# A fused attention and feed-forward block: another order of the work, the first quarter split in its bank, and the last two masks added by VectorE

## The chip, the cores and the metric
One core of a Trainium2 chip. The metric is the device time of one execution in microseconds (us). TensorE multiplies, VectorE, ScalarE and GpSimd work on elements, and SyncE's queue issues the DMAs. PSUM is the memory that TensorE writes, in banks of 128 x 512 f32; SBUF is the memory for the rest.

## The reference
With x of 2 x 1024 tokens and C = 128, all in f32:
```
xn  = layernorm(x)
q3, k3 = xn @ Wq.T, xn @ Wk.T              # 8 heads of 3 dimensions
v   = xn @ Wv.T                            # 8 heads of 16
scores = (q3 . k3) * scale + (q3 . dir_h) * (k3 . dir_h)
attn = softmax(where(causal, scores, -inf));  A = (attn @ v) @ Wo.T
h   = bitlinear(xn, w_fc) + gate * (xn @ v'.T @ fast_b.T @ u.T)
F   = bitlinear(relu(h)**2, w_proj)        # ternary weights times a scale, hidden size 512
out = x + A + F
```

## The kernel before
**Tiling.** The 2048 tokens are four quarters of 512. Attention is made in eight chunks: batch, group of four heads, and which half of the batch's tokens the queries are (`CHUNKS`). Chunks 0, 1, 6 and 7 have queries in a first half (four steps of 128 keys, all crossing the diagonal, of 512, 384, 256 and 128 queries), chunks 2 to 5 in a second half (four full steps of 512, then four such).

**A chunk.** Its `max` units make scores on TensorE (queries on the partitions, K=32 rows of bf16, line 875), and VectorE takes their least values: a plain reduce where no mask is needed (line 576), and an addition of `mask_row` with a reduce (line 579) on the diagonal. (The scores are negated, so that a minimum stands for the softmax's maximum.) Chunks 0, 1, 6, 7 have 12 units, the others 28, of which 16 are plain ones. `top` and `prep` write the minima as three bf16 parts beside the queries, and a transpose (`maxT`) puts them on the other axis. Then for each step and pair of heads `st` (line 903) makes the scores with the keys on the partitions and the maximum subtracted, ScalarE takes the exponential (line 729), and `pv` (line 927, 8 matmuls in f32) adds to `obank`. `oT`, `oB` and `y` turn, divide and project.

**The diagonal, in chunks of `BOUNDED`** (all eight before): scores over the diagonal could overflow, so ScalarE first applies a Relu to the first 128 columns of both heads of the pair (`late`, line 715), and after the exponential GpSimd sets what lies over the diagonal to zero (`causal`, line 446); `pv` waits for GpSimd. In a chunk outside `BOUNDED`, VectorE adds the tile `late` (a large number over the diagonal) to the scores in their bank, and `pv` waits for the exponential alone.

**q and k** are split in three bf16 parts each (`qkv`, `split`, `spread`), and laid in the tile X with repeats. For quarters 1 to 3 GpSimd does it and a DMA transposes X. For quarter 0 the path is: ScalarE casts the first part (line 675), VectorE subtracts it from the bank into the SBUF tile `rest` (line 528), casts that (532), subtracts again (534), and ScalarE and VectorE copy the parts to X (691, 539); TensorE transposes X (`rows`, line 842), and ScalarE copies the result to QK (695).

**The feed-forward part**: `ffn`, `ffn2` (lines 850, 855; 2 matmuls of 128x512 in f32 each), Relu, square on GpSimd, and `hid` (763), which shares its bank with `y`.

**The order.** Each engine runs its items in the order of one list, `ORDER`. `WEAVE` is that list with a letter for each stream (M maxima, A `st`, O `late` of bounded chunks, K `late` of the others, G exponentials, D `causal`, P `pv`, H `ffn`, B `hid`, Y `oB` and `y`, and so on); each letter takes the next item of its stream. Engines wait for each other by semaphores only. The `max` units have three banks (`VB`), `st`, `ffn` and `qkv` two double banks (`AB`). `IDLE` puts matmuls on zeros ahead of four items of TensorE's (12 before `weights wqk`, 7 before `xT 0`, 2 before `qkv 0`, 6 before `rows 0 0`); they don't wait for the item's own operands.

Of the kernel before, what the change touches and what calls it, by code (L numbers as in the profile page):

```python
# [21 lines left out]
G = H // HG  # L22
# [83 lines left out]
BOUNDED = (0, 1, 2, 3, 4, 5, 6, 7)  # L106
# [65 lines left out]
NNWNNWCXFNUNWQCFIULNENVUNNMMEMHMMMNHSMMXMJMXQIVMMQNLHMMEVMMHRMMHMMHMMTXMJMMAOMHMGMHMMSMMRAAMOMMGOHGMAIMMOHMGMM  # L172
AMOAMGMMMAOOTMGMGDAAODMOGMMGAOMAMMPMDDMGMOAPMGSAOSGPOLRMGMAMADOTGOPADGOMMPDGHMMHMQVMMADMAPEIMAMPMAMMAMPAMPPJLM
AAMPAOMGMAOMEMAMMPMGMADORGPMOGAOMMMADPGMOMAGMAPOOGMMGTADMADMAMMAMAMSMAMAMMAMMAMMAOMOPGGMAMMOGMAPDPOAPMGMMROAGO
PDTAGPAMMOGODGMAPMMAAMPADMMMAPMAMAMPAMMPPMAMPHOMGHHMMHMAMMOPMMAMGOPRMMAPMGMOAPMMGOADPGOGAMTMOADOGBSGAAYMBAYMAD
PAMDMMPPAMPBAAMBAMYOAPGOGMAPOSGRMAOMPDMMGAPAOTDMGMOMGAOPAGPOGMAMADOBODPPGARGBDYABOSGYOAGOAPOGBBATGDAOYOGBAGAOP
ODDGBAGDOPABGPYOPGPAOAOGGYBAOYGDAPPDPOGDPBPBBYYY
# [23 lines left out]
def build(nc, x, Wq, Wk, Wv, Wo, scale, fast_b, w_fc, w_proj, u, v, gate, consts, out):  # L201
# [3 lines left out]
    with ctx:  # L205
# [258 lines left out]
        def _(dve):  # L464
# [12 lines left out]
            for item in ORDER:  # L477
# [36 lines left out]
                elif item == ("xn", 0):  # L514

                    dve.wait_ge(rstd_ready, 1)
                    for n in range(TPC):
                        last = nc.vector.tensor_scalar(xn[:, n, :], x_sb[:, n, :], mv[:, n, 0:1], rstd[:, n:n + 1],
                                                       ALU.subtract, ALU.mult)
                    last.then_inc(xn_ready, 1)  # L520
                elif item == ("weights", "wqk"):
                    nc.vector.tensor_copy(wall[:, C:VQK], filled(item)[:, 0:2 * NQ]).then_inc(free(item), 1)
                elif kind == "qkv":
# [111 lines left out]
        def _(act):  # L635
# [9 lines left out]
            for item in ORDER:  # L645
# [31 lines left out]
                elif kind == "v":  # L677
# [4 lines left out]
                    act.wait_ge(res_ready, q + 1)  # L682
                    if q == 0:
                        act.wait_ge(ones_ready, 1)
                    nc.scalar.copy(V[:, q * TPC:(q + 1) * TPC, :, 0:HD],  # L685
                                   qkv_view(unit)[:, :, 0:C].rearrange("p n (h d) -> p n h d", d=HD)).then_inc(free(unit), 1)
                elif item == ("spread", 0):
                    for k, ready in ((0, hi_ready), (1, mid_ready)):
                        act.wait_ge(ready, 1)
                        for side in range(2):  # L690
                            last = nc.scalar.copy(*part_rows(0, side, k))
# [285 lines left out]
```

## Time and profile before
| | |
|---|---|
| runs | 171.37 us (median of 170.3, 171.37, 173.21) |
| the profiled execution | 172.44 us, its span 169.8 us |
| TensorE busy | 155.9 us |
| VectorE busy | 133.6 us |
| ScalarE busy | 123.0 us |
| GpSimd busy | 67.5 us |
| mean granted clock of TensorE | 0.91 |

The span goes from the first to the last instruction of the profiled execution. The granted clock is 1.00 at 2.4 GHz and 0.50 at 1.2 GHz. "Busy" for TensorE includes matmuls that overlap in the pipeline.

### The profile page before, as it was taken

Reading aid. Unit: us, or ns where it says so; the run is one execution under the profiler, and the core shown is the slowest. Engines: PE = TensorE matmul, PEld = TensorE weight load, DVE = VectorE, ACT = ScalarE, POOL = GpSimd, SP = SyncE. Lnnn points to the kernel's source line nnn. Section 1 sums busy time; section 2 is a strip of 40 time slices with the busy share of each in tenths; the row PEclk is TensorE's granted clock in tenths of the full one; section 3 lists DMA queues with packets and bytes.
Section 4 is the critical chain, followed back from the end, with each engine's and each line's share of the span. In section 5 each row is a group of like instructions: output and inputs, shape, how many; then the busy total and the mean of one; then the engine's idle time right before and its main releaser. Section 6 shows DMA issues by size and latency. Waiting matters only on the chain.

```text
span 169.8 us, 3241 instructions
## 1 busy us (share of the span) xinstructions
PE 155.9 (92%) x1080; PEld 63.1 (37%) x1081; DVE 133.6 (79%) x435; ACT 123.0 (72%) x218; POOL 67.5 (40%) x119
## 2 busy tenths in 40 slices
PE   6995999898879988898889999999999999999993
PEld 2452627232212124232122221242255523785772
DVE  0899659899999899899999796899995867150541
ACT  1556764858578674999889776986879898969810
POOL 8064004999415992702450151000492223832310
PEclk9999559999975599999995558999999999999999
DMA  3850000060100016090100010000011020021012
GB/s 96 201 180 2 0 0 4 0 124 2 31 0 8 0 31 124 0 127 0 31 0 4 0 33 2 0 4 0 0 35 31 0 66 0 0 62 37 11 52 62
DMA packets 16764, 5.76 MB, mean 34 GB/s; under 512 B 11308, under 2 KB 16620, under 8 KB 16748
## 3 DMA queue, kind: packets, MB, share of 16 engines
q1 hardware_dynamic: 16352, 5.41, 14.8%
q10 hardware_dynamic: 396, 0.16, 0.3%
q8 instruction: 8, 0.13, 0.3%
q14 instruction: 8, 0.07, 0.1%
HBM read 2.02 MB, written 1.05 MB: 18 GB/s over the span
## 4 chain that ended last, share of the span: by engine, by line
PE 54%; DVE 31%; ACT 8%; issue 3%; DMA 2%; SPq 1%; ACTq 0%; DVEq 0%
PE obank L927 16%; DVE pm L576 11%; DVE vbank L579 10%; PE vbank L875 9%; PE vbank L763 9%; PE abank L903 6%; ACT Pr L729 6%; PE abank L850 5%; PE abank L855 4%; DMA k_sb<-in_consts 2%; PE vbank L947 2%; ACT abank L715 2%; DVE pm L579 2%; DVE stats L484 1%; PE abank L842 1%
## 5 line engine op out<-in xcount | busy, mean ns | idle before, releaser
L729 ACT ACTIVATE Pr<-abank 128x1024 f32<-128x1024 f32 (+3 forms) x96 | 74.5, 814 | 6.9 <-PE abank L903 1.9
L579 DVE CUSTOM_DVE_ANT_0 vbank<-vbank,mask_row 128x128 f32<-128x128 f32 (+3 forms) x128 | 58.8, 523 | 7.9 <-PE vbank L875 7.6
L875 PE MATMUL vbank<-QK 32*128 32x512 bf16 (+3 forms) x192 | 47.5, 364 | 3.4 <-DVE pm L576 1.7
L927 PE MATMUL obank<-Pr,V 128*32 128x512 f32 (+3 forms) x384 | 43.5, 544 | 0.2 <-issue 0.2
L576 DVE TENSOR_REDUCE pm<-vbank 128x1 f32<-128x512 f32 x64 | 39.5, 681 | 3.2 <-PE vbank L875 3.0
L446 POOL TENSOR_SCALAR_AFFINE_SELECT Pr<-Pr 128x512 f32<-128x512 f32 x32 | 20.1, 637 | 49.9 <-ACT Pr L729 49.6
L903 PE MATMUL abank<-QK 32*128 32x512 bf16 (+3 forms) x192 | 33.9, 358 | 3.2 <-ACT Pr L729 1.9
L875 PEld LDWEIGHTS vbank<-QK 32*128 32x128 bf16 x192 | 12.5, 94 | 49.7 <-issue 20.1
L715 ACT ACTIVATE abank<-abank 128x256 f32<-128x256 f32 x64 | 23.6, 375 | 9.8 <-PE abank L903 9.0
L437 POOL TENSOR_TENSOR r<-r 128x1024 f32<-128x1024 f32 x8 | 15.1, 1895 | 11.4 <-ACT r L709 11.4
L579 DVE DVE_READ_ACCUMULATOR2_ANT pm<- 128x1 f32 x128 | 18.0, 141 | 0.0
L763 PE MATMUL vbank<-w2T,r 128*128 128x128 f32 x128 | 17.5, 284 | 0.0
L903 PEld LDWEIGHTS abank<-QK 32*128 32x128 bf16 x192 | 8.7, 92 | 22.0 <-ACT Pr L729 13.4
L763 PEld LDWEIGHTS vbank<-w2T,r 128*128 128x128 f32 x128 | 15.3, 191 | 2.8 <-issue 2.4
L709 ACT ACTIVATE r<-abank 128x1024 f32<-128x1024 f32 x8 | 8.2, 1024 | 9.0 <-PE abank L855 9.0
L927 PEld LDWEIGHTS obank<-Pr,V 128*32 128x32 f32 x384 | 8.8, 113 | 11.6 <-issue 9.9
L611 DVE STREAM_TRANSPOSE oT<-obank 128x512 f32<-128x512 f32 x8 | 5.7, 710 | 7.1 <-PE obank L927 7.1
L850 PE MATMUL abank<-xnT,w1T 128*128 128x512 f32 x16 | 9.8, 700 | 0.6 <-ACT V L685 0.4
L456 POOL CAST X<-nmax 128x16 bf16<-128x16 f32 x8 | 2.1, 257 | 20.6 <-DVE nmax L595 16.8
L631 DVE TENSOR_TENSOR xn<-vbank,x_sb 128x256 f32<-128x256 f32 x8 | 3.4, 424 | 8.5 <-PE vbank L947 8.4
L855 PE MATMUL abank<-xnT,w1T 128*128 128x512 f32 x16 | 9.8, 698 | 0.0
L769 PE MATMUL obank<-mask_row 128*128 128x512 bf16 x26 | 7.9, 445 | 1.3 <-POOL mask_row L388 1.3
(101 smaller groups left out, 127.8 us busy)
## 6 DMA issues: line engine op xcount, KB each, us to landing
x_sb<-in_L_attn_x SPq DMA_DIRECT2D x4, 256.0 KB, 3.6
out_y<-xn SPq DMA_DIRECT2D x8, 128.0 KB, 1.8
wfc_sb<-in_L_ffn_w_fc SPq DMA_DIRECT2D x1, 256.0 KB, 4.1
wpj_sb<-in_L_ffn_w_proj SPq DMA_DIRECT2D x1, 256.0 KB, 3.0
QK<-X SPq DMA_TRANSPOSE x10, 2.5
k_sb<-in_consts SPq DMA_DIRECT2D x2, 64.0 KB, 3.2
Wv_sb<-in_L_attn_Wv ACTq DMA_DIRECT2D x1, 64.0 KB, 3.5
Wo_sb<-in_L_attn_Wo ACTq DMA_DIRECT2D x1, 64.0 KB, 4.0
```

Source lines behind the costliest of these rows:

```text
L437: nc.gpsimd.tensor_tensor(r, r, r, ALU.mult).then_inc(r2_ready, 1)
L446: nc.gpsimd.affine_select(diagonal, diagonal, [[0, HG], [1, P]], ALU.is_ge, 0.0, base=0, channel_multiplier=-1).then_inc(causal_done, 1)
L576: last = nc.vector.tensor_reduce(out=least, in_=s_n, op=ALU.min, axis=AX.X)
L579: last = nc.vector.tensor_tensor_reduce(out=s_n, in0=s_n, in1=mask_row[:, CH - keys:CH], scale=1.0, scalar=3.0e38, op0=ALU.add, op1=ALU.mi ...
L715: nc.scalar.activation(scores, scores, ACT.Relu).then_inc(bounded, 1)
L729: nc.scalar.activation(Pr[:, n % PSLOTS, 2 * pair:2 * pair + 2, 0:cols], src[:, :, 0:cols], ACT.Exp, scale=-1.0).then_inc(free(unit), 1)
L763: nc.tensor.matmul(o[:, at:at + P], r2[:, j, t:t + P], w2T[:, j, :], start=j == 0 and at == 0, stop=False)
L850: nc.tensor.matmul(o[:, 0, :], w1T[:, j * P:(j + 1) * P], xnT[:, q * CH:(q + 1) * CH], start=True, stop=True)
L855: nc.tensor.matmul(bank(unit)[:, 1, :], w1T[:, j * P:(j + 1) * P], xnT[:, q * CH:(q + 1) * CH], start=True, stop=True).then_inc(full(unit), 1)
L875: last = nc.tensor.matmul(o[:, at:at + keys], QK[r, quarter(b, chunk), 0, g, q0:q0 + P], QK[r, quarter(b, half), 1, g, 0:keys], start=True ...
L903: last = nc.tensor.matmul(o[:, n, 0:cols], QK[r, quarter(b, j // TPC), 1, g, k0:k0 + P], QK[r, quarter(b, chunk), 0, g, first:CH], start=T ...
L927: last = nc.tensor.matmul(obank[32 * h:32 * h + 32, first:CH], V[:, b * TPB + j, HG * g + h, :], Pr[:, n % PSLOTS, h, 0:cols], start=step ...
```

## The change
Four edits.

1. `BOUNDED` loses chunks 6 and 7. Their 16 Relus of ScalarE (8 each) become 16 additions of VectorE in the banks, and their 8 `causal` items of GpSimd are gone.
2. The first quarter's split. VectorE's residual stays in the bank. ScalarE casts the middle part from there, with the copies of the first part to X before and behind it; VectorE subtracts the middle part from the bank. V's copy out of the bank waits for that.
3. `xn 0` releases its four tiles one by one, and the transposes of `xT 0` wait for each.
4. `WEAVE` is another list.

```diff
-BOUNDED = (0, 1, 2, 3, 4, 5, 6, 7)
+BOUNDED = (0, 1, 2, 3, 4, 5)
...
+        def qk_rest():
+
+            return qkv_view(("qkv", 0))[:, :, C:VQK].rearrange("p t (s c) -> p t s c", s=2 * G)
...
-                        last = nc.vector.tensor_scalar(xn[:, n, :], x_sb[:, n, :], mv[:, n, 0:1], rstd[:, n:n + 1],
-                                                       ALU.subtract, ALU.mult)
-                    last.then_inc(xn_ready, 1)
+                        nc.vector.tensor_scalar(xn[:, n, :], x_sb[:, n, :], mv[:, n, 0:1], rstd[:, n:n + 1],
+                                                ALU.subtract, ALU.mult).then_inc(xn_ready, 1)
...
-                    nc.vector.tensor_tensor(rest(q), src, bf16_part(q, 0),
+
+                    nc.vector.tensor_tensor(rest(q) if q else src, src, bf16_part(q, 0),
                                             ALU.subtract).then_inc(res_ready, 1)
                 elif item == ("split", 0):
-                    dve.wait_ge(res_ready, 1)
-                    nc.vector.tensor_copy(bf16_part(0, 1), rest(0)).then_inc(mid_ready, 1)
                     dve.wait_ge(mid_ready, 1)
-                    nc.vector.tensor_tensor(bf16_part(0, 2), rest(0), bf16_part(0, 1),
+                    nc.vector.tensor_tensor(bf16_part(0, 2), qk_rest(), bf16_part(0, 1),
                                             ALU.subtract).then_inc(lo_ready, 1)
...
-                    act.wait_ge(res_ready, q + 1)
                     if q == 0:
+                        act.wait_ge(lo_ready, 1)
                         act.wait_ge(ones_ready, 1)
+                    else:
+                        act.wait_ge(res_ready, q + 1)
...
+                elif item == ("split", 0):
+                    act.wait_ge(hi_ready, 1)
+                    nc.scalar.copy(*part_rows(0, 0, 0))
+                    act.wait_ge(res_ready, 1)
+                    nc.scalar.copy(bf16_part(0, 1), qk_rest()).then_inc(mid_ready, 1)
+                    nc.scalar.copy(*part_rows(0, 1, 0))
                 elif item == ("spread", 0):
-                    for k, ready in ((0, hi_ready), (1, mid_ready)):
-                        act.wait_ge(ready, 1)
-                        for side in range(2):
-                            last = nc.scalar.copy(*part_rows(0, side, k))
+                    act.wait_ge(mid_ready, 1)
+                    for side in range(2):
+                        last = nc.scalar.copy(*part_rows(0, side, 1))
                     last.then_inc(laid_act, 1)
```

What the new list does to TensorE's order at the places that matter (`max c u` is unit u of chunk c):
```
start, before: wqk | xT 0, lora_u, wvo, qkv 0, lora_b, rows 0 0, w1, max 0 0-1, rows 0 1, max 0 2, ffn 0, max 0 3-5, ffn2 0
start, after:  wqk | wvo, xT 0, lora_u, qkv 0, lora_b, rows 0 0, rows 0 1, max 0 0-1, w1, max 0 2-7, xT 1, max 0 8-9, xT 2,
               qkv 1, max 0 10-11, qkv 2, max 1 0-1, ffn 0, ...
chunk 2's maxima, before: ffn 4, ffn2 4 by unit 11, then units 12-27 with st of chunk 0 and 1, then pv 0 0
chunk 2's maxima, after:  ffn 3, 4 and their ffn2 by unit 14, pv 0 0 behind unit 19, pv 0 1 behind 22, pv 0 2 behind 26,
                          then max 3 0-9 with st of chunk 1, pv 0 3, st 2 0 0, max 3 10-11, qkv 3, max 3 12-13, st, pv 1 0
chunk 4's maxima, before: pv 2 1 to 2 4 by unit 8, then units 9-25 with st of chunk 3, pv 2 5, ..., pv 2 6, pv 2 7
chunk 4's maxima, after:  pv 2 1 to 2 5 by unit 14, then units 15-27 and max 5 0 with st of chunk 3, pv 2 6, pv 2 7
end, before: ... y 3 0, hid 2 0 0, st 7 3 0, y 3 1, st 7 3 1, pv 7 0-3, hid 2 0 1, hid 2 1 0, hid 2 1 1, y 2 0, y 2 1
end, after:  ... hid 2 0 0, st 7 2, pv 7 0-1, st 7 3, y 3 0, y 3 1, pv 7 2-3, hid 2 0 1, hid 2 1 0, hid 2 1 1, y 2 0, y 2 1
```
VectorE now has `rstd 1` behind `max 0 1` and not before `max 0 0`, and in chunks 6 and 7 the additions stand between `max 7 10`, `top 7`, `oT 5`, `y 1`, `oB 3` and `oT 6`, in the order of the scores. ScalarE has V's copy and `lora_b` ahead of the first `rows`.

## Rows read from the trace of the kernel before

**Rows 1.** Windows of the whole span: busy us (instructions) per engine, granted clock, DMA.
```profile
17.84:24.66 6.82, 6.82 (x27) 2.81 (x26) 4.29 (x24) 4.62 (x11) 0.00 (x0) 0.50 0.00 0
24.66:48.56 23.90, 21.53 (x101) 8.67 (x100) 22.64 (x70) 16.53 (x27) 15.63 (x26) 1.00 0.15 28
48.56:58.80 10.24, 9.67 (x48) 2.04 (x48) 9.98 (x37) 7.28 (x16) 6.65 (x8) 0.50 0.01 3
58.80:89.52 30.72, 27.05 (x210) 8.28 (x206) 29.12 (x71) 25.35 (x42) 14.09 (x29) 1.00 0.28 43
89.52:103.17 13.65, 13.49 (x76) 3.02 (x76) 11.70 (x41) 10.80 (x18) 2.91 (x7) 0.50 0.05 11
103.17:144.00 40.83, 40.25 (x345) 14.58 (x342) 34.44 (x119) 34.50 (x54) 11.29 (x19) 1.00 0.06 14
144.00:169.80 25.80, 23.03 (x228) 16.84 (x226) 8.83 (x21) 14.86 (x31) 8.01 (x14) 1.00 0.14 37
84.90:89.50 4.60, 4.09 (x27) 1.11 (x23) 4.60 (x8) 3.99 (x6) 2.50 (x2) 1.00 0.00 0
```

**Rows 2.** The chain that ended last, middle and end: start us, us, what.
```profile
79.90 9.74 DVE pm L576 x16
...
94.38 1.44 PE obank L927 x8
...
99.60 1.90 PE obank L927 x8
...
122.13 0.99 PE obank L927 x8
...
163.27 2.87 PE vbank L763 x24
```

**Rows 3.** Timeline of the start: start us, us, engine, line, operation.
```profile
6.37 1.69 PE L769 MATMUL obank<-mask_row 128*128 128x512 bf16 x7
...
7.36 0.29 POOL L398 COPY Wo_by_head<-Wo_sb 128x128 f32<-128x128 f32 x1 [3.03 <-DMA Wo_sb<-in_L_attn_Wo]
...
7.89 0.60 PE L821 MATMUL abank<-k_sb,xn 128*128 128x128 f32 x4
...
10.13 1.43 PE L831 MATMUL abank<-wall,xnT 128*128 128x176 f32 x8 [0.37 <-ACT wall L734]
...
11.60 0.32 ACT L675 CAST r<-abank 128x192 bf16<-128x192 f32 x1 [1.61 <-PE abank L831]
...
12.23 0.35 DVE L528 TENSOR_TENSOR r<-abank,r 128x192 f32<-128x192 f32 x1
...
12.62 1.08 DVE L532 CAST r<-r 128x192 bf16<-128x192 f32 x1
13.15 1.76 ACT L691 COPY X<-r 128x288 bf16<-128x288 bf16 x4
...
13.73 1.18 DVE L534 TENSOR_TENSOR r<-r 128x192 bf16<-128x192 f32 x1
...
16.29 1.01 ACT L695 CAST QK<-abank 128x1024 bf16<-128x1024 f32 x1 [1.38 <-PE abank L842]
...
17.23 1.56 PE L806 MATMUL vbank<-k_sb,wfc_sb 128*128 128x128 f32 x8
...
18.53 0.17 DVE L512 SCALAR_TENSOR_TENSOR shift<-mv,rstd 128x12 f32<-128x12 f32 x1
...
19.40 0.30 DVE L579 CUSTOM_DVE_ANT_0 vbank<-vbank,mask_row 128x128 f32<-128x128 f32 x1 [0.70 <-PE vbank L875]
...
23.09 0.30 DVE L579 CUSTOM_DVE_ANT_0 vbank<-vbank,mask_row 128x128 f32<-128x128 f32 x1 [1.68 <-PE vbank L875]
```

**Rows 4.** Groups by form: busy us, mean ns, idle before.
```profile
L715 ACT ACTIVATE abank<-abank 128x256 f32<-128x256 f32 x64 | 23.6, 375 | 9.8 <-PE abank L903 9.0
...
L446 POOL TENSOR_SCALAR_AFFINE_SELECT Pr<-Pr 128x512 f32<-128x512 f32 x32 | 20.1, 637 | 49.9 <-ACT Pr L729 49.6
...
L631 DVE TENSOR_TENSOR xn<-vbank,x_sb 128x256 f32<-128x256 f32 x8 | 3.4, 424 | 8.5 <-PE vbank L947 8.4
```

More of the change, by code:

```diff
@@ L171 @@
 WEAVE = """
[L172 to L177, printed above, removed]
+NNWNCNWFWFNXUQILNVUECNNEMMUNMNMMMMMNXMMXJQIVMMQVMMMLHNMERMHJMMHMMIMHMMXMTMHMMMHAMMOMHLMSMGHMMMAMHMOMGAOMGHMRMM
+DAMTAOOMGPSDAGMMOAOMGDPMAMGMAOMPGDOGAOMMMMARGOAOMGMMAMGMOGAOGEDMDAMMOAGTOPPMGAMQVMMAPMMAPMDAMAMDPILMAMPMPAJHMM
+EHAMMAMMMPOAMMGOAMPMOGAMGMAOPGOGMMAOGMARPDMAOGDOTMGDAMPMAMAMPMDAMAMSMAMMAMAMMAMMAOMGSMOGMAOMPDGPAPMMOMARPSOGAT
+GDAMMOOGPGAMOGMAPADMMMAPDAYMMAPMAMMAPAMMPAMOPGPHMMHAMSPAMOMGPOMMAGPOMMAPGMRDAMOGOGMHMTAOHMMDGMPDAOPMGDAMPAMPMA
+MBAAPMBAYBAMAMBAYMAOGYPAMMOMPSGAMPROMGAOGMOPMDAGMODTMASPGOPAGDAKMBOGAGPKADBGKBGAAMKPGKBBAGPAKGKYRYBAKGTABGAPKK
+PGGPYAAKPBKGBGPAAKGPKPAKGGAKYGYPPPYBBBYY
 """
@@ L815, in _ @@
                     o = empty(item)
-                    pe.wait_ge(xn_ready, q + 1)
                     if q == 0:
                         pe.wait_ge(ld_id, 16)
+                    else:
+                        pe.wait_ge(xn_ready, TPC + q)
                     for n in range(TPC):
+                        if q == 0:
+                            pe.wait_ge(xn_ready, n + 1)
                         last = nc.tensor.transpose(o[:, 0, n * P:(n + 1) * P], xn[:, q * TPC + n, :], ident)
```

## The prediction

> **What bounds the kernel now.** I read the windows first, cut where TensorE's granted clock changes, then the chain that ended last, then the start. Busy shares of the whole span don't name one limit, since the limit changes on the way; [rows 1] is the map. Up to 17.84 us the clock is at its upper level, 2.4 GHz, and the work is a thin path through all engines. From 17.84 to 24.66 it is at 1.2 GHz (0.50), and VectorE is busy for 4.29 of 6.82 us. From 24.66 to 89.52, VectorE is busy for 22.64 of 23.90, 9.98 of 10.24 and 29.12 of 30.72 us: the row maxima set the pace, and the 10.24 us at half clock in the middle hide almost wholly behind them. In the third half-clock stretch, 89.52 to 103.17, VectorE falls to 11.70 of 13.65 us and TensorE is at 13.49. From there to the end TensorE is full (40.25 of 40.83 us, then 23.03 of 25.80, with the closing store in it), and VectorE isn't (34.44, then only 8.83 of 25.80). So: a path, then VectorE, then from about 94 us TensorE alone.
>
> The chain says the same of the end: it runs from matmul group to matmul group, and closes with 24 matmuls of the hidden layer, 2.87 us [rows 2]. The eight matmuls of a full `pv` step take 0.99 us in it at 2.4 GHz and 1.90 us at 1.2 [rows 2]. Before the clock fell at 89.52 TensorE had run only K=32 matmuls for 4.6 us: 27 of them, 4.09 us busy, none of lines 927, 850 or 763 [rows 1]. "Busy" did not keep the clock. Three such falls cost TensorE half of 6.82 + 10.24 + 13.65 = 30.7 us, 15.4 us of its work, but the end sees only the part where TensorE is the limit: in the third stretch from about 94.4 us on, where the chain becomes TensorE's [rows 2], (103.17 − 94.4) / 2 = 4.4 us.
>
> **The masks of chunks 6 and 7.** Removed: 16 Relus of ScalarE (64 in all take 23.6 us, 0.375 each [rows 4]), 6.0 us, and 8 of GpSimd's 32 selects at 0.637 us [rows 4], 5.1 us with their wait. Added: 16 additions of VectorE on 128x256 elements in PSUM. The trace has none; nearest is the 128x256 addition of line 631, 0.424 us [rows 4]. So 16 x 0.42 = 6.8 us, with bounds of 0.38 (the Relu's own time) and 0.5. VectorE has room: after 144 us it is busy for 8.83 of 25.80 us [rows 1], and 8.8 + 6.8 is still under two thirds. Who waits: `exp` behind the addition, and the additions behind `oT`, `oB` and `y` on VectorE. In the new order each of those that waits for TensorE has the matching matmuls ahead of the scores that the next addition needs, and two or more hidden-layer groups (24 matmuls in 2.87 us, 0.96 a group [rows 2]) lie beside it. Since the chain of this stretch has no GpSimd and almost no ScalarE, taking 11 us from them gives nothing by itself. I book −0.2 us, bounds −1 and +1.5 (a few scores late by one addition each, 0.42, with nothing behind to fill in). The end is the same three hidden groups over `oT` and `oB`, so nothing there.
>
> The Trainium skill ("VectorE: DVE Perf Modes", the section on the TRN2 errata) speaks against this move: it gives a PSUM source 172 + N cycles at 1.2 GHz on ScalarE and 120 + N at 0.96 GHz on VectorE. That is an estimate of 0.36 and 0.39 us for N = 256, the Relu being the cheaper. By it the 16 additions would be 6.3 us, and the sum wouldn't change.
>
> **The first quarter's split.** Before, the residual goes to SBUF, and VectorE casts it (1.08 us) and subtracts again (1.18 us), while the same 128x192 subtraction out of the bank took 0.35 us [rows 3]. Now ScalarE casts from the bank (0.32 us, as the first part [rows 3]), and VectorE subtracts from the bank (0.35 us). Saved on the path: 1.08 + 1.18 − 0.32 − 0.35 = 1.6 us; and VectorE no longer stands in a `var` when the first part is ready, 11.60 + 0.32 = 11.92, 12.23 − 11.92 = 0.3 us. But three of ScalarE's four copies into X (1.76 us for four, 0.44 each [rows 3]) now lie behind the middle part's cast, against VectorE's two of the last part before: X is laid about 0.5 us later than VectorE alone would give. V's copy and lora_b's, both 512 columns wide, now also stand ahead of the copy of the first rows on ScalarE; by the 1.01 us of that copy of 1024 columns [rows 3] an estimated 1.1 us, partly under the rows' matmuls, about 0.5 us more. Net −0.9 us, bounds −1.6 and 0.
>
> Both slow SBUF instructions ran while GpSimd worked on the ternary weights. The Trainium skill ("GPSIMD Engine Reference", the table of the engine's interfaces) says that it shares its SBUF interfaces with VectorE where VectorE has two SBUF inputs or a two-port mode. The long times agree with that, and by it the bank version should be free of it; the durations above already say so.
>
> **Order at the start.** `xn` now releases each tile, so the transposes could start earlier. But TensorE's `weights wvo` is now ahead of `xT 0`, and needs Wo's copy of GpSimd, which ends at 7.36 + 0.29 = 7.65 us [rows 3]; and the seven clock-keeping matmuls (1.69 us [rows 3]), which ran beside the wait for `xn`, are tied to `xT 0`. They now come after 8.0 us. Transposes end near 8.0 + 1.5 + 0.5 = 10.0 us against 8.49. Since `qkv 0` waited until 10.13 for the copy of `wall` [rows 3], only some 0.6 us of that is seen. So the first rows are copied at about 16.29 − 0.9 + 0.6 = 16.0 us. Now `w1` (until 18.79 [rows 3]) doesn't stand ahead of the first maxima: VectorE starts on them near 17.3 instead of 19.40 us. Of these 2.1 us, 1.2 go to `rstd 1`, six small instructions of 0.17 us and more with their gaps [rows 3], which VectorE now has after two units instead of before them, and `w1` (2.5 us, up to 4 at half clock) now stands behind two units. VectorE has about 2.4 us of work to cover it, so a wait of 0 to 2 us stands there, in place of the one of 1.68 us at 23.09 [rows 3]. The ffn matmuls are moved out of chunk 0 behind `qkv 2`; that takes away two waits, but leaves TensorE light while the clock is low, so that `qkv 1` may run at half speed (1.43 us at full [rows 3], so +1.4). Sum for everything before chunk 2's maxima: −0.5 us, bounds −2.6 and +1.5.
>
> **Order in the middle.** Reading the orders by items: before, 16 maxima units separate `ffn2 4` from `pv 0 0`, and 17 units `pv 2 4` from `pv 2 5`, the two light stretches in or before which the clock fell. After, `pv 0 0` to `pv 0 2` are drawn into chunk 2, so the first has 5 units, but a new light one of 11 units lies between `pv 0 2` and `pv 0 3`; the second has 14 units, between `pv 2 5` and `pv 2 6`. Both are of the kind that preceded the fall at 89.52 [rows 1], K=32 matmuls alone; at 0.61 us a unit (16 took 9.74 us [rows 2]) they last 6.7 and 8.5 us. So I expect three falls again: the second behind `pv 0 2`, some 7 us later on the work's own scale than before, the third some 3 us later. What sets their price is how densely full-width matmuls stand behind them. Behind the second: one short `pv`, then `qkv 3` and `pv 1 0`; it ended before with two `pv`. VectorE's idle time there was 0.26 of 10.24 us [rows 1]; I book +0.5 us, bounds −0.3 and +5 (the rival). Behind the third: the fall comes nearer to the point where TensorE is the limit, but the low clock has then less light work to outlast; if it ends at the same `pv 3 1`, the loss of 4.4 us shrinks by about a quarter. I book −1.2 us, bounds −4.4 (no loss at all) and +4 (another such stretch).
>
> **The sum.** −0.2 − 0.5 + 0.5 − 1.2 = −1.4 us. The profiled execution took 172.44 us, 2.64 us around its span of 169.8; it would become 171.0. The median of the runs, 171.37, lies 1.07 us under it, so the forecast is 170.0 us, no measurable change: about 2% is what a measurement of this kernel can tell (168.0 to 174.8).
>
> **Rivals.** (A) The low clock ends early or doesn't come. For: the heavy work of chunks 0 to 2 is spread more evenly, 5 units instead of 16 in the first gap. Against: 11 and 14 units in a row remain. Then the 4.4 us go, with the start's 0.5: 171.37 − 4.9 = 166.5 us. Chance 20%. (B) The other side: the low clock of the second stretch outlasts `qkv 3` and `pv 1`. Between `pv 0 3` and `ffn 5` the full-width matmuls are 1.43 us of `qkv 3`, 2.5 us of four `pv` (0.99 us for 512 columns [rows 2], scaled for 384, 256 and 128) and 0.6 of `w2`'s four transposes, as `xT`'s [rows 3]; at half clock these and the K=32 matmuls between them take some 5 us more than VectorE's maxima can hide. In the chain before, it took 8.8 us of half clock from `pv 2 5` on to get out. It decides if a light group stands between any two `pv` there, which the new order has. Time: 170.0 + 5 = 175.0 us, chance 16%. (C) The change doesn't do what it says: the start's gain goes into the wait for Wo and for `w1`, the falls stay as long, and the masks are hidden: 171.4 us, chance 20%. The forecast itself, 168.5 to 171.5, has 40%, and 4% is left for worse than (B): both stretches long, near 180.
>
> **How the numbers follow.** Faster by over 2% is (A): 0.20. Slower is what of (B) lies past 174.8, about two thirds as its price is open upwards, and the rest: 0.15. Within: 0.65. The range reaches from 166.3 to 175.0, leaving out a tenth at each end. The bounds of the small terms (−1 and +1.5 of the masks, −2.6 and +1.5 of the start) lie within it.
>
> **What would show it.** First maxima of VectorE at 17.3 us, two waits for TensorE in the 8 us after. The split's subtraction of the last part at 0.35 us. Three half-clock stretches, the third starting after chunk 4's last score groups. From `pv 3 0` on TensorE without gaps, VectorE's 16 additions at 0.42 us, and no wait of ScalarE for them of over 0.5 us. The forecast is wrong above all if the stretches at 1.2 GHz sum to well under or over 31 us: each 2 us more where TensorE is the limit is 1 us of time.

## The result

| | before | after |
|---|---|---|
| median of the runs | 171.04 us (4 runs, 170.3 to 173.21) | 175.35 us (4 runs, 173.83 to 175.94) |
| the profiled execution, its span | 172.44, 169.8 us | 174.85, 173.1 us |
| mean granted clock of TensorE | 0.91 | 0.892 |
| half-clock stretches (start + length, us) | 17.84 + 6.82, 48.56 + 10.24, 89.52 + 13.65 | 18.45 + 10.24, 56.00 + 10.24, 90.13 + 17.07 |

The ratio of the times is 1.025, with a 95% interval of 1.016 to 1.035: the change made the kernel slower by about 4 us. Here and below a median is that of all runs, while a ratio leaves out the runs over 1.5% above the shortest of their kernel. The head of the page of after, then the windows, cut as those of before at each change of the clock (against [rows 1]; the last row is a part of the end):
```profile
PE 156.9 (91%) x1080; PEld 64.7 (37%) x1081; DVE 139.3 (80%) x450; ACT 118.2 (68%) x203; POOL 62.8 (36%) x111
...
PEclk9999656999999558999995556999999999999999
```
```profile
18.45:28.69 10.24, 9.76 (x38) 6.05 (x37) 8.19 (x38) 5.83 (x14) 0.16 (x1) 0.50 0.00 1
...
56.00:66.24 10.24, 9.90 (x45) 3.90 (x42) 9.24 (x19) 7.49 (x15) 3.55 (x8) 0.50 0.07 14
66.24:90.13 23.89, 21.03 (x177) 6.11 (x173) 23.00 (x68) 21.22 (x32) 10.96 (x18) 1.00 0.15 29
90.13:107.20 17.07, 16.20 (x88) 3.36 (x90) 14.27 (x35) 11.61 (x21) 7.27 (x10) 0.50 0.04 9
107.20:144.00 36.80, 36.03 (x313) 12.50 (x309) 31.51 (x114) 30.99 (x47) 10.10 (x18) 1.00 0.06 16
144.00:173.10 29.10, 23.76 (x233) 17.07 (x230) 14.82 (x36) 11.31 (x18) 1.77 (x6) 1.00 0.12 33
151.30:158.20 6.90, 4.32 (x38) 3.22 (x42) 2.69 (x8) 2.28 (x4) 0.00 (x0) 1.00 0.23 57
```
The last 29.1 us hold about the TensorE work that took 25.8 before (23.76 us busy against 23.03 [rows 1]), and the last row has much of the difference: for 6.9 us no engine is near full, and TensorE stands for 2.6 of them. The chain that ended last names the two places that decided the case (start us, us, what), and ends as before with 24 hidden-layer matmuls [rows 2]:
```profile
97.77 2.02 DVE on L617
...
153.40 2.44 DMA QK<-X
...
166.57 2.87 PE vbank L772 x24
```
A transfer stands in the chain near the end, where before there was only TensorE, and a VectorE instruction of 2.02 us near 98 us. The timeline of after round the first of these, cut to the engines that matter (start us, us, engine; SPq is SyncE's queue, with the instruction that issues a DMA):
```profile
147.06 0.26 POOL L460 CAST X<-nmax 128x16 bf16<-128x16 f32 x1 [1.40 <-DVE nmax L600]
...
148.03 0.27 POOL L463 TENSOR_TENSOR X<-nres,X 128x16 bf16<-128x16 f32 x1
...
152.03 0.77 DVE L633 TENSOR_TENSOR xn<-vbank,x_sb 128x256 f32<-128x256 f32 x2
152.47 0.89 SPq L378 DMA_DIRECT2D out_y<-xn  x2
...
153.40 1.20 SPq L370 DMA_TRANSPOSE QK<-X  x1
...
155.97 0.39 PE L915 MATMUL abank<-QK 32*128 32x512 bf16 x2 [2.58 <-DMA QK<-X]
```
`prep 7` is done at 148.30, yet its transpose `maxT 7` is issued at 153.40: in the new list it stands behind `y 1 0` and `y 1 1`, whose stores SyncE issues, and SyncE waits for their last additions at 152.03. TensorE stands 2.58 us at `st 7 0 0`. The same place before: the transpose lay between the two stores.
```profile
149.24 0.37 SPq L374 DMA_DIRECT2D out_y<-xn  x1
149.66 1.20 SPq L366 DMA_TRANSPOSE QK<-X  x1
...
152.67 0.37 SPq L374 DMA_DIRECT2D out_y<-xn  x1
```
The other place, in the timeline of after:
```profile
97.60 1.89 POOL L441 TENSOR_TENSOR r<-r 128x1024 f32<-128x1024 f32 x1
97.77 2.01 DVE L617 TENSOR_TENSOR on<-oT,inv 128x256 f32<-128x256 f32 x1
```
The multiplication of `oT 2` by `inv`, two inputs in SBUF, is 0.42 us when alone (below); here it ends 0.29 us behind GpSimd's square of the ffn beside it. In before's trace the same instruction took 0.72 us, beside a 0.64 us select:
```profile
99.48 0.64 POOL L446 TENSOR_SCALAR_AFFINE_SELECT Pr<-Pr 128x512 f32<-128x512 f32 x1
...
99.68 0.72 DVE L615 TENSOR_TENSOR on<-oT,inv 128x256 f32<-128x256 f32 x1
```

**Where the time went.** Stages measured from the first instruction of one item to that of another, from the timelines (us); for a `max` unit that is VectorE's, for a `pv` step TensorE's:

| kernel | start to `max 2 0` | to `max 4 0` | to `max 5 0` | to `max 5 8` | to `pv 5 0` | to `pv 7 3` | to the end |
|---|---|---|---|---|---|---|---|
| before | 39.71 | 40.19 | 18.14 | 8.16 | 28.75 | 27.91 | 6.96 |
| after | 39.02 | 38.85 | 18.27 | 10.61 | 29.36 | 30.06 | 6.96 |
| difference | −0.69 | −1.34 | +0.13 | +2.45 | +0.61 | +2.15 | 0 |

The start and the middle gained 2.0 us. The stages of `max 5` and of the end lost 4.6, and their causes had to be found. The +0.61 between them is there with the new list whatever the clock (29.4 us, and 30.2 in `t_zeros23`, against 28.7 to 28.8 with the old list), and stayed unexplained.

How the 2.0 us divide over the first two stages is a matter of this one pair of profiles. Three more kernels below run the old list unchanged up to `max 4 0`: `b_masks`, `b_masks_near` and `b_zeros3`. They reached `max 2 0` at 37.3 to 37.6 us and `max 4 0` at 79.3 to 79.7. The twelve profiles with the new list reached them at 37.4 to 39.5 and at 75.9 to 78.1. So the gain up to `max 4 0` is there in all of them, 1.1 us at least, but a gain up to `max 2 0` is not shown.

### The profile page after: what moved, and what is told of

The parts are those of the page before. It is cut to its first block, busy times and chain, and to the rows that moved or that the text cites. A ratio compares the mean times of both kernels' runs of the same rounds, so it can differ in the third digit from the quotient of the medians.

```text
span 173.1 us, 3235 instructions
## 1 busy us (share of the span) xinstructions
PE 156.9 (91%) x1080; PEld 64.7 (37%) x1081; DVE 139.3 (80%) x450; ACT 118.2 (68%) x203; POOL 62.8 (36%) x111
## 3 DMA queue, kind: packets, MB, share of 16 engines
HBM read 2.02 MB, written 1.05 MB: 18 GB/s over the span
## 4 chain that ended last, share of the span: by engine, by line
PE 46%; DVE 29%; ACT 13%; issue 5%; DMA 4%; ACTq 2%; SPq 0%; DVEq 0%
DVE vbank L581 12%; PE obank L939 11%; ACT Pr L738 9%; DVE pm L578 8%; PE vbank L772 8%; PE vbank L887 6%; PE abank L843 5%; PE abank L915 4%; PE abank L862 4%; PE abank L867 3%; DMA Wo_sb<-in_L_attn_Wo 2%; DVE pm L581 2%; ACT abank L724 2%; PE abank L833 1%; DMA QK<-X 1%
## 5 line engine op out<-in xcount | busy, mean ns | idle before, releaser
L738 ACT ACTIVATE Pr<-abank 128x1024 f32<-128x1024 f32 (+3 forms) x96 | 74.0, 813 | 17.0 <-DVE abank L589 10.3
L887 PEld LDWEIGHTS vbank<-QK 32*128 32x128 bf16 x192 | 12.0, 93 | 42.0 <-issue 14.7
L450 POOL TENSOR_SCALAR_AFFINE_SELECT Pr<-Pr 128x512 f32<-128x512 f32 x24 | 15.4, 645 | 30.6 <-ACT Pr L738 30.4
L724 ACT ACTIVATE abank<-abank 128x256 f32<-128x256 f32 x48 | 17.9, 376 | 6.9 <-PE abank L915 6.6
L772 PE MATMUL vbank<-w2T,r 128*128 128x128 f32 x128 | 17.0, 282 | 0.0
L589 DVE TENSOR_TENSOR abank<-abank,k_sb 128x256 f32<-128x256 f32 x16 | 6.4, 430 | 10.5 <-PE abank L915 10.5
L939 PEld LDWEIGHTS obank<-Pr,V 128*32 128x32 f32 x384 | 8.6, 113 | 12.9 <-issue 11.1
L862 PE MATMUL abank<-xnT,w1T 128*128 128x512 f32 x16 | 8.9, 635 | 0.5 <-ACT Pr L738 0.4
L867 PE MATMUL abank<-xnT,w1T 128*128 128x512 f32 x16 | 9.0, 644 | 0.0
L433 POOL COPY X<-r 128x288 bf16<-128x288 bf16 x18 | 8.3, 542 | 0.4
```

What stands on the lines that cost most here:

```text
L450: nc.gpsimd.affine_select(diagonal, diagonal, [[0, HG], [1, P]], ALU.is_ge, 0.0, base=0, channel_multiplier=-1).then_inc(causal_done, 1)
L724: nc.scalar.activation(scores, scores, ACT.Relu).then_inc(bounded, 1)
L738: nc.scalar.activation(Pr[:, n % PSLOTS, 2 * pair:2 * pair + 2, 0:cols], src[:, :, 0:cols], ACT.Exp, scale=-1.0).then_inc(free(unit), 1)
L772: nc.tensor.matmul(o[:, at:at + P], r2[:, j, t:t + P], w2T[:, j, :], start=j == 0 and at == 0, stop=False)
L862: nc.tensor.matmul(o[:, 0, :], w1T[:, j * P:(j + 1) * P], xnT[:, q * CH:(q + 1) * CH], start=True, stop=True)
L867: nc.tensor.matmul(bank(unit)[:, 1, :], w1T[:, j * P:(j + 1) * P], xnT[:, q * CH:(q + 1) * CH], start=True, stop=True).then_inc(full(unit), 1)
```

## The experiments

Ratios are to the kernel before in the same batch, with 95% intervals (before there: 171.63 us in 13 runs, 171.53 in 30, 171.48 in 17, 171.13 in 20). `a_` starts from after, `b_` from before, and `t_` from after with `maxT 7` moved as in the first.

**1. The queue of SyncE (`a_turn`, `a_turn_again`).** Only `T` (`maxT 7`) moves ahead of `y 1 0`:
```diff
-...AKGKYRYBAKGTABGAPKK
+...AKGKTYRYBAKGABGAPKK
```


> The changed kernel with one item moved: the transpose of chunk 7's maxima stands ahead of both output stores of quarter 1 on SyncE, not behind them. Theory (queue): in the changed kernel TensorE stood still for 2.58 us behind this DMA, which was issued 5 us after its operands were ready because the queue waited for y 1 1. Then about 2 to 2.6 us of the 4.3 us of loss go: ratio to the kernel before 1.010 to 1.014, and no wait of TensorE for the DMA in the trace. Rival (TensorE's work is the bound anyway, the wait is filled from elsewhere, or the mask additions are what holds the end): under 0.7 us, ratio 1.02 or more.

Measured 170.06 us (167.66 to 172.06, 4 runs), ratio 0.980 (0.966 to 0.994). The same kernel again in another batch, with 6 runs:

> a_turn once more, as the measure for the other three on the same chip. Its four runs went from 167.7 to 172.1 us. The theory that totals differ by where the half-clock stretches fall: in the profile, pv 5 0 to pv 7 3 is 27.25 us again, and what differs from the first profile lies in stretches at 0.50.

171.2 us (168.93 to 172.1), ratio 0.989 (0.983 to 0.996). In both profiles the stage from `pv 5 0` to `pv 7 3` fell from 30.06 to 27.25 us. In the second, whose clock fell much as after's (89.86 + 17.07 us), the stage before it and the one of `max 5` stayed (29.37 and 10.60), so its gain of 3.3 us of span is the queue's 2.8 and 0.5 of the first two stages. The first also had the third half-clock stretch short:
```profile
90.65:97.48 6.83, 6.57 (x39) 1.56 (x39) 6.63 (x15) 5.59 (x10) 3.51 (x7) 0.50 0.10 19
```
VectorE is at 6.63 of 6.83 us in it: such a stretch costs little. The two profiles of this one kernel are 3.9 us apart, all of it in the stages that hold the half-clock stretches (1.0, 0.5 and 2.45 us).

The wait can cost more than 2.8 us. `a_square` and `t_square` (experiment 6) are a second pair that differs in this one move, timed in the same batch: 172.78 against 168.42 us, and the stage 31.62 against 27.25 us, 4.4 us each. In `a_square` the clock fell behind the wait:
```profile
153.33:156.74 3.41, 3.41 (x17) 1.50 (x19) 1.16 (x3) 2.02 (x2) 0.00 (x0) 0.50 0.02 5
```
In after's profile it didn't. In how many of after's runs it did is not on record; the two medians of this kernel lie 5.3 and 4.15 us under after's.

**2. The masks, in the new order (`a_bound`, `t_bound`, `t_bound_late`).** `BOUNDED` back to all eight, `K` back to `O`, `D` behind the exponentials:
```diff
-BOUNDED = (0, 1, 2, 3, 4, 5)
+BOUNDED = (0, 1, 2, 3, 4, 5, 6, 7)
```


> The changed kernel with all eight chunks in BOUNDED: the last two masks by ScalarE's Relu and GpSimd's select again, in the same order, each select right behind its two exponentials. Theory (queue and clock): the masks were worth little, so the time stays within 1 us of the changed kernel, ratio 1.02 to 1.03. Rival (the additions of VectorE hold the end): 1.5 us or more faster than the changed kernel, ratio 1.016 or less. A third way, that the masks by VectorE were worth something behind this order: slower than the changed kernel by over 1 us.

176.97 us (174.9 to 178.57, 4 runs), ratio 1.021 (1.007 to 1.036). As a total it looks like "the masks don't matter"; the profile says otherwise, the stage to `pv 7 3` being 33.92 us against 30.06. Of this a part is a half-clock stretch (157.86 + 3.41 us) behind a wait of 3.50 us for the same transpose. With `maxT 7` moved as well:

> a_bound (masks of the last two chunks by ScalarE and GpSimd) with the transpose ahead of the stores: what the masks by VectorE are worth in the new order without the wait in SyncE's queue. Theory: nothing, within 1 us of a_turn (170 us). Rival, that VectorE's additions cost: faster than a_turn by 1 us or more. Rival, that they help since pv no longer waits for GpSimd: slower by 1 us or more. The profile, from pv 5 0 to pv 7 3, decides where the clock makes the totals scatter: 27.25 us in a_turn.

179.27 us (175.72 to 180.05, 6 runs; no interval could be given). Its timeline shows why this is no fair price of the masks:
```profile
152.51 0.63 POOL L450 TENSOR_SCALAR_AFFINE_SELECT Pr<-Pr 128x512 f32<-128x512 f32 x1 [1.84 <-ACT Pr L738]
153.09 0.25 POOL L460 CAST X<-nmax 128x16 bf16<-128x16 f32 x1
...
156.89 0.39 PE L915 MATMUL abank<-QK 32*128 32x512 bf16 x2 [3.48 <-DMA QK<-X]
```
Here too the clock fell behind the wait (158.47 + 3.41 us). I had put the selects of chunk 6 ahead of `prep 7` on GpSimd, and `prep 7` began 5 us too late. So once more, with three selects (`causal 6 0` to `6 2`) behind `prep 7`:
```diff
-...AOGDOTYRYBAOGABGD...
+...AOGOTYRDDDYBAOGABGD...
```


> t_bound with the first three selects of chunk 6 behind prep 7 on GpSimd, as the kernel before has it; in t_bound prep 7 stood behind them, and the transpose came 3.5 us late. A fair measure of the masks in the new order. Theory: pv 5 0 to pv 7 3 falls from 33.95 us to between 28.5 and 31, against 27.25 with the masks by VectorE: they are worth 1.3 to 3.7 us there, since the order puts each pv right behind its scores. Rival (the whole loss of t_bound was that one queue): 27.5 us or less. Other rival (the selects in front of pv cost all of it): 33 us or more.

171.92 us (170.54 to 174.02, 10 runs), ratio 1.004 (0.999 to 1.009); the stage is 29.89 us, against 27.25 with the masks by VectorE, both at full clock. In the new order, then, the masks by VectorE are worth 2.6 us of this stage. That is for this placement of Relus and selects; before's own took 27.91.

**3. The masks alone, in the old order (`b_masks`, `b_masks_near`).** First with each addition where its Relu stood:
```diff
-BOUNDED = (0, 1, 2, 3, 4, 5, 6, 7)
+BOUNDED = (0, 1, 2, 3, 4, 5)
 (WEAVE: the O of chunks 6 and 7 become K, their 8 D go)
```


> The kernel before with the change of the masks alone: BOUNDED without chunks 6 and 7, its order kept, the 8 selects taken out. Theory: TensorE is full in that stretch, so ratio 0.995 to 1.005. Rival (the additions cost, queued behind oT, oB and y on VectorE): 1.01 or more.

174.41 us (174.27 to 175.83, 4 runs), ratio 1.018 (1.009 to 1.028). The stage to `pv 7 3` took 31.77 us, +3.9. The timeline shows the addition for `st 6 1 1` behind an instruction of `y 1 0`, which waits for TensorE, and ScalarE behind both:
```profile
147.97 0.42 DVE L631 TENSOR_TENSOR xn<-vbank,x_sb 128x256 f32<-128x256 f32 x1 [2.45 <-PE vbank L947]
148.32 0.76 DVE L587 TENSOR_TENSOR abank<-abank,k_sb 128x256 f32<-128x256 f32 x2
...
148.86 1.30 ACT L729 ACTIVATE Pr<-abank 128x768 f32<-128x768 f32 x2 [2.41 <-DVE abank L587]
```
Then with each addition right behind its scores in the list:

> b_masks (the kernel before with the masks by VectorE) with each of the 16 additions right behind its scores in the list, so that none stands on VectorE behind a y, oB or oT that waits for later matmuls of TensorE. Theory: in b_masks the loss of 3.9 us from pv 5 0 to pv 7 3 (31.77 against 27.91) was such queueing; here that stretch is 28.5 us or less, the ratio 1.00 to 1.008. Rival (the addition's own 0.43 us and the engine changes cost in themselves): 30.5 us or more, ratio 1.015 or more.

172.3 us (171.28 to 174.01, 10 runs), ratio 1.004 (0.999 to 1.008); the stage 29.07 us. So 2.7 of the 3.9 us were the place in VectorE's queue. Of the 1.2 that remain, one wait of that kind is seen, two additions at 159.95 for which ScalarE waited 2.59 us:
```profile
159.95 0.76 DVE L587 TENSOR_TENSOR abank<-abank,k_sb 128x256 f32<-128x256 f32 x2
160.50 1.08 ACT L729 ACTIVATE Pr<-abank 128x512 f32<-128x512 f32 x2 [2.59 <-DVE abank L587]
```

**4. The first quarter's split alone (`b_split`).** After's code with before's list and before's `BOUNDED`.

> The kernel before with the first quarter's split in the bank and the tile by tile release of xn alone, in the old order. Theory: the first rows are laid 0.9 us or more earlier, but w1's matmuls on TensorE still stand ahead of the first maxima; VectorE's first maximum 0.5 to 1 us earlier than 19.4, and time 0 to 1 us lower, ratio 0.994 to 1.0. Rival: nothing earlier at all since ScalarE's copies take the place of VectorE's, ratio 1.0 to 1.005.

171.27 us (170.04 to 175.78, 11 runs), ratio 1.001 (0.995 to 1.007): no difference. Its own instructions are as short as in after (subtraction 0.36 us, cast 0.32), but its profiled execution, with 175.52 us, was one of the longest and began its first maximum at 20.57 us. The split can be read on its own stretch alone, from the cast of the first part to the first `rows` matmuls: 4.04 us before (11.60 to 15.64), 3.63 here (12.41 to 16.04) and 3.03 in after (12.20 to 15.23).

**5. The clock's third stretch (`t_zeros3`, `t_zeros23`, `b_zeros3`).** With `maxT 7` moved, one full-width matmul of zeros into `obank` ahead of each of `max 4 16` to `max 5 0`, 13 in all:
```diff
+            def add_zeros(n):
+
+                zeros = mask_row[:, 0:CH // 2].bitcast(bf16)
+                for _ in range(n):
+                    nc.tensor.matmul(obank[:, :], zeros[:, 0:P], zeros, start=False, stop=False)
...
+                if item in ZEROS:
+                    add_zeros(ZEROS[item])
```


> a_turn (the changed kernel with the transpose ahead of the stores) with 13 matmuls that add zeros to obank in full width (128 rows, 512 columns of bf16, about 0.22 us each), one ahead of each max unit from 4 16 to 5 0, the third stretch without other full-width work. The output is unchanged. Theory (clock): the third half-clock stretch, 6.8 to 17.1 us long in the profiles so far, goes away; the granted clock stays 1.00 from the second stretch on, TensorE saves 2 to 6 us from pv 3 0 on, median 167 us or less, and the runs scatter less. Rival (13 matmuls more of TensorE's time, 2.8 us, in a stretch where it is nearly full, or the clock falls all the same): 170 us or more.

172.0 us (169.91 to 172.71, 12 runs), ratio 1.001 (0.998 to 1.005). The same with ten more, ahead of `max 3 0` to `3 9`; and the 17 ahead of `max 4 9` to `4 25` in the kernel before:

> As t_zeros3, with 10 such matmuls more, one ahead of each unit of max 3 0 to 3 9, the stretch between pv 0 2 and pv 0 3. Theory: the second half-clock stretch goes too; VectorE is the limit there, so another 0.5 to 2 us, median 165 to 166.5 us. Rival: the second stretch was hidden behind VectorE; the same as t_zeros3 within 0.5 us, or slower by TensorE's 2.2 us.

171.45 us (170.21 to 173.3, 12 runs), ratio 0.998 (0.995 to 1.001).

> The kernel before with 17 such matmuls of zeros, one ahead of each unit of max 4 9 to 4 25, its light stretch before the fall of the clock at 89.5 us. Theory: no half-clock stretch there; 2 to 5 us faster than the kernel before, ratio 0.97 to 0.99. Rival: the low clock was hidden behind VectorE, ratio 0.995 to 1.01.

171.99 us (169.47 to 176.57, 12 runs), ratio 0.995 (0.991 to 0.999). Half a per cent in the old order. In the new order the ratios must be held against those of `a_turn`, the same kernel without zeros, 0.980 and 0.989: with the 13 zeros it is 1 to 2% slower, and the intervals don't meet. The theory that the zeros would win back the loss fell. `t_zeros23` also answers for the second stretch. In its profile the clock held from 27.58 to 102.67:
```profile
27.58:102.67 75.09, 68.38 (x434) 21.73 (x435) 71.69 (x204) 58.93 (x98) 39.54 (x68) 1.00 0.15 29
```
Yet it reached `max 4 0` at 77.48 us, within the 75.9 to 78.1 of the kernels that had this stretch: it was hidden behind VectorE, as the rival said. The windows of the first, then its timeline, show what they did:
```profile
65.87:103.42 37.55, 33.16 (x252) 9.50 (x251) 35.86 (x100) 31.28 (x49) 15.87 (x26) 1.00 0.13 22
103.42:106.83 3.41, 3.41 (x25) 0.47 (x21) 1.93 (x4) 1.81 (x4) 2.05 (x2) 0.50 0.00 0
```
```profile
98.77 2.00 DVE L618 TENSOR_TENSOR on<-oT,inv 128x256 f32<-128x256 f32 x1
...
101.55 0.39 PE L896 MATMUL vbank<-QK 32*128 32x512 bf16 x1 [1.34 <-DVE pm L579]
```
The clock held through chunk 4's maxima, where it had fallen at 90 us, and fell at 103.42, behind the place where TensorE stood 1.34 us for VectorE, which was held up by the 2.00 us multiplication. The zeros took 0.74 us for themselves (`max 4 16` to `max 5 0` 8.50 against 7.76 us).

**6. The square beside the multiplication (`a_square`, `t_square`).** This led to the next edit: `S` (`square 4` on GpSimd) moves from behind `prep 4` ahead of `causal 3 4`, where GpSimd stood idle for 6 us. Once on after as it is, once with `maxT 7` moved:
```diff
-...OMAOMPDGPAPMMOMARPSOGAT
+...OMAOMPSDGPAPMMOMARPOGAT
```


> The changed kernel with one item moved on GpSimd: square 4 (the multiplication of 128x1024 elements, 1.89 us) stands ahead of causal 3 4, where GpSimd was idle for 6 us, and not behind prep 4. Theory (GpSimd and VectorE get in each other's way): in all kernels with the new order the VectorE multiplication of oT 2, 0.43 us elsewhere, took 2.0 us, until the 1.89 us multiplication of GpSimd beside it had ended. Then it takes 0.43 us here, and from max 5 0 to max 5 8 (10.61 us in the changed kernel) 1.6 us go; the time is 173.5 to 174.5 us. Rival (TensorE at half clock is the limit there, so VectorE's 1.6 us were covered): the instruction is short but the stretch is not, under 0.4 us.

172.78 us (170.51 to 174.58, 12 runs), ratio 1.006 (1.002 to 1.011), against 1.025 for after.

> a_turn with the same move of square 4. Theory: 1.0 to 1.6 us faster than a_turn on the same chip; max 5 0 to max 5 8 from 8.15 to about 6.6 us where the clock is full at its end. Rival: no difference beyond 0.3 us.

168.42 us (165.97 to 169.45, 6 runs), ratio 0.974 (0.967 to 0.981). The multiplication in `a_square`, and the wait for the transpose, which this kernel keeps:
```profile
96.77 0.42 DVE L617 TENSOR_TENSOR on<-oT,inv 128x256 f32<-128x256 f32 x1
...
150.03 1.20 SPq L370 DMA_TRANSPOSE QK<-X  x1
...
152.58 0.39 PE L915 MATMUL abank<-QK 32*128 32x512 bf16 x2 [2.58 <-DMA QK<-X]
```
2.0 us have become 0.42, and against the kernels without the move the medians fall by 2.6 (175.35 to 172.78) and 2.8 us (171.2 to 168.42). The two last were timed in one batch. Both falls are more than the instruction's 1.6 us; the profiles of these kernels also differ in their half-clock stretches.

**7. All three (`t_square_zeros3`).** `t_square` with the 13 zeros:

> t_zeros3 with the same move of square 4. In t_zeros3 the clock stayed up through the light stretch and fell at 103.4 us instead, after TensorE had waited 1.34 us for VectorE behind the 2.0 us multiplication. Theory: without that wait the third fall is gone altogether, the time 2 to 3.5 us under t_zeros3 (172.0), thus 168.5 to 170, and under t_square if its third stretch reaches past pv 3 0. Rival: the fall comes anyhow, as TensorE also waits for oT 2 there.

168.16 us (167.59 to 168.32, 6 runs), ratio 0.980 (0.976 to 0.984). From the window row of its middle, no stretch at half clock is left from 66.51 to 144:
```profile
66.51:144.00 77.49, 74.04 (x609) 25.21 (x607) 68.23 (x218) 66.07 (x101) 28.29 (x47) 1.00 0.09 18
```
The median is that of `t_square` within the scatter (168.42), and by the ratios the zeros gain nothing here either (0.974 without them); the runs lie closer together. `max 5 0` to `max 5 8` takes 6.67 us here, with the clock up and the square away. That is the measure for the others (the second column goes from `max 5 0` to the end of the stretch; in after that is past the end of the stage):

| kernel | half clock from `max 5 0` on, us | square beside `on` | the stage, us | over 6.67 |
|---|---|---|---|---|
| `t_square` | 3.6 | no | 7.05 | 0.4 |
| `a_turn` | 3.3 | yes | 8.15 | 1.5 |
| `a_square` | 7.0 | no | 8.22 | 1.5 |
| after | 11.1 | yes | 10.61 | 3.9 |

From the first two, with about the same clock, the square costs 1.1 us; as the instruction alone it is 2.01 − 0.42 = 1.6. That leaves 2.3 to 2.8 of after's 3.9 us to the low clock, by subtraction. The old list has its own measure: in `b_masks` and `b_split`, whose third stretch ended before `max 5 0`, the stage took 7.22 and 7.20 us, against before's 8.16 with 5.1 us of half clock.

**8. The start (`t_start`).** `t_square` with the 13 zeros, and `W` (`wvo`) behind `xT 0`, as before:
```diff
-NNWNCNWFWFNXUQ...
+NNWNCNWFFNXWUQ...
```


> t_square_zeros3 (168.2 us) with one item moved: weights wvo behind xT 0 on TensorE and ScalarE, as the prediction priced it: the seven clock-keeping matmuls run beside the wait for xn again. Theory: the transposes end 1.2 us earlier, qkv 0 starts 0.5 us earlier (10.2 against 10.71), VectorE's first maximum at 17.1 instead of 17.6, and 0 to 0.5 us of the end. Rival: a wait for Wo elsewhere eats it, no change.

167.2 us (166.78 to 167.95, 4 runs), ratio 0.975 (0.969 to 0.982). In its timeline the transposes end at 9.36 us, and `qkv 0` starts at 10.40 against 10.73 in after:
```profile
8.76 0.60 PE L842 MATMUL abank<-k_sb,xn 128*128 128x128 f32 x4
...
10.40 1.43 PE L852 MATMUL abank<-wall,xnT 128*128 128x176 f32 x8
```
Its median is the lowest of all, 2.5% under the kernel before. That this edit gained is not shown: the interval overlaps those of `t_square` (0.974) and `t_square_zeros3` (0.980), the median's lead of 1 us is between batches, and the profiles show 0.3 us at `qkv 0` and 0.15 at the first maximum (17.46 against 17.61).

## Why the prediction was wrong

The forecast was 170.0 us; the median is 175.35, just over the upper end of the range. The prediction said for the masks "nothing there" at the end and booked −0.2 us, and this is **the step that failed**: for the end it followed the new list on the engines that compute, and not along SyncE's queue, where the list put a transpose behind two stores. That stage lost 2.15 us. A second term had the wrong sign: the third half-clock stretch, booked at −1.2 us, cost 1.4 to 1.9 us more than before. And an item moved on GpSimd's queue, the square, was in no term. By stages (span): the end came 2.35 us over its term, `max 5` 3.65 over the third stretch's, the middle 1.8 under the second stretch's and the start 0.2 under; 0.7 us lie in stages that had no term. That is the 4.7 us between the −1.4 booked and the +3.3 measured.

**SyncE's queue, +2.8 us, and 4.4 where the clock fell behind the wait.** `maxT 7` went behind the stores of `y 1 0` and `y 1 1`. Shown by moving it back alone (30.06 to 27.25 us, twice). Without it the end would be 0.66 us shorter than before (27.91), near the booked −0.2 and within its bounds. The term's bound of +1.5 was for "a few scores late by one addition each"; a DMA behind an instruction that waits was not in it.

**GpSimd's queue, +1.1 to 1.6 us.** `square 4` moved behind `prep 4`, and there runs beside `on`. Shown by moving it: 2.01 to 0.42 us, and 2.6 to 2.8 us of the median, in which the clock may have a part. The prediction even had the mechanism: it cited the Trainium skill ("GPSIMD Engine Reference", the table of the engine's interfaces) for the sharing of SBUF's interface where VectorE has two SBUF inputs, but used it only for the instructions that the change removed. It was not asked where the new list puts such a pair together.

**The masks' instructions** were well sized: 16 additions, foreseen at 0.42 us each with bounds of 0.38 and 0.5. The line of after:
```profile
L589 DVE TENSOR_TENSOR abank<-abank,k_sb x16: 422/432/433, 144.2 to 164.9; 128x256 f32<-128x256 f32 x16
...
  ACT Pr L738: 10.3, 9
```
The Trainium skill's cost for PSUM sources ("VectorE: DVE Perf Modes", the TRN2 errata), by which I had estimated 0.39 us, is under the measured 0.43; its figure is for results that go to SBUF, while these stay in PSUM. ScalarE waited for the additions nine times, 10.3 us in all, one of the marks that the prediction gave against itself ("no wait of ScalarE for them of over 0.5 us"); in `a_turn` it was 7.6 us in eight waits, and TensorE had no gap there. TensorE had hidden-layer groups, and the stage is the shortest with the additions in the new order (27.25 against 29.89 us). So "taking 11 us from them gives nothing by itself" was wrong in that order, by 2.6 us for the one placement tried, and in the old order the same move costs 3.9 us or 1.2, by place.

**The third stretch**, booked at −1.2 us, went the other way. It began at 90.13, where expected, but lasted 17.07 instead of 13.65 us, and ended at 107.20 instead of 103.17, behind the point from which TensorE is the limit. Its part in the stage of `max 5` is 2.3 to 2.8 us by subtraction. Before's stage took 8.16 us, and the old list at full clock 7.2 (`b_masks`, `b_split`), so its low clock cost 0.95 us. The term was then +1.4 to +1.9 and not −1.2, and its base was too large: the prediction put the loss of the stretch before at 4.4 us, counting TensorE as the only limit from 94.4 us on. A stretch costs little while VectorE's maxima last, and more the further it reaches behind them (3.6, 7.0 and 11.1 us from `max 5 0` on: 0.4, 1.5 and 2.3 to 2.8). That it lengthened because TensorE had waited for VectorE behind the long multiplication fits `t_zeros3` (the fall at 103.42 behind such a wait) and `t_square_zeros3` (none); for after itself it isn't shown, since `a_turn` has the same multiplication and only 6.83 us. The stretches sum to 37.6 us, not the 31 foreseen, and in runs of one kernel they lie differently: the kernel before with added zeros took 169.47 to 176.57 us in 12 runs.

**The second stretch** was booked at +0.5. It came behind `pv 0 2` at 56.00, 7.4 us later (some 7 foreseen), with VectorE idle for 1.0 of 10.24 us; but from `max 2 0` to `max 4 0` the kernel won 1.34 us, outside the bounds on the good side. Rival (B), which would have given nearly the measured time, is refuted for this profile: the low clock ended at 66.24, behind `qkv 3` (63.08 to 65.79) and ahead of `pv 1 0` (66.27), and did not outlast `pv 1`. That the stretch itself was hidden is shown by `t_zeros23`. What in the order wins there I did not test.

**The start** came as predicted in its instructions, and its total partly by luck. Three terms of it in after's timeline, with the price of the wait for Wo:
```profile
7.92 1.67 PE L778 MATMUL obank<-mask_row 128*128 128x512 bf16 x7
...
10.73 1.43 PE L843 MATMUL abank<-wall,xnT 128*128 128x176 f32 x8
...
13.30 0.36 DVE L536 TENSOR_TENSOR r<-abank,r 128x192 bf16<-128x192 f32 x1 [0.39 <-ACT r L695]
...
13.70 1.39 DVE L541 COPY X<-r 128x288 bf16<-128x288 bf16 x2
...
15.88 1.01 ACT L704 CAST QK<-abank 128x1024 bf16<-128x1024 f32 x1 [0.28 <-PE abank L854]
...
17.77 0.30 DVE L581 CUSTOM_DVE_ANT_0 vbank<-vbank,mask_row 128x128 f32<-128x128 f32 x1
```
`qkv 0` starts 0.60 us later than before (0.6 booked), the first rows are copied at 15.88 (16.0), the first maximum is at 17.77 (17.3), and up to `max 2 0` the kernel gained 0.69 us (0.5). The last part's subtraction takes 0.36 us. The split gained 1.0 us on its own stretch (4.04 to 3.03 us; 0.9 booked). Of the two waits for TensorE foreseen in the 8 us behind the first maximum one came, 0.62 us at 24.36. But the profile of before was a late one: the old list began its first maximum at 18.56 to 18.80 us in `b_masks`, `b_masks_near` and `b_zeros3`, against 19.40, and reached `max 2 0` about 2 us earlier, with no half-clock stretch before 41 us. All twelve profiles with the new list have such a stretch beginning between 17.3 and 22.4 us. So up to `max 2 0` the new start shows no gain over the old one in general. That the two copies to X take 1.39 us was not foreseen; before they took 0.55, once GpSimd's multiplications had ended. Here GpSimd's last one, 1.14 us, starts at 13.72, beside them; they end 0.23 us behind it.

**Against the rivals**: (A) did not come, (B) gave the number without its mechanism, and (C) did not come either, with a loss clear of the scatter; no gain at all is what the split alone gives (ratio 1.001).

## What to carry to other kernels

When a list orders all engines, walk the new one along every queue, those that issue DMAs first: for each item that moved, ask what it is now behind, when that is released, and who waits for the item. A transfer behind a store that waits for other work is late by that wait, here 5.1 us, of which TensorE stood still for 2.58, and the clock can fall behind it; the busy rows of the engines hardly tell (TensorE 155.9 and 156.9 us). And check pairs as well as orders: an item moved to a place of its engine where it runs beside a VectorE instruction on SBUF can lengthen that, with no wait of its own in the trace; compare the longest with the shortest instance of a group of one form.

## What the runs showed of the hardware

A VectorE multiplication of 128x256 with two inputs in SBUF took 0.42 us with GpSimd idle, 0.72 beside a 0.64 us select, and 2.0 us beside GpSimd's 128x1024 multiplication of 1.89 us (in after, `a_turn`, `a_turn_again` and `t_zeros3` alike). In after and `a_turn` it ended 0.29 us behind GpSimd's instruction, and beside the select of before 0.28 us behind it (99.48 + 0.64 against 99.68 + 0.72, rows of the timeline). With GpSimd's instructions of such different length (0.64 and 1.89 us) the same 0.28 to 0.29 us were left behind them, so it was not slowed in proportion, but held until the other was nearly or wholly done. And zeros multiplied on TensorE, which kept the clock up where they stood, gained half a per cent in the old order (0.995) and went with 1 to 2% more time in the new one (1.001 and 0.998 against 0.980 and 0.989 without them): in `t_zeros3` they moved the fall to the next wait.
